# Both feed-forwards of an audio tower written out over all groups, and the fp4 weight work spread over groups 1 to 7

## The reference, cut to what matters

```python
# third stage, L0_ffn (w1q, w3q, w2q: weights rounded to -s, 0, s); x is a layer-normed row block
h1 = jnp.einsum('bsd,hd->bsh', x, w1q)          # 512 -> 1365
h3 = jnp.einsum('bsd,hd->bsh', x, w3q)
g = jax.nn.silu(h1) * h3
return jnp.einsum('bsh,dh->bsd', g, w2q)        # 1365 -> 512

# fifth stage, L1_ffn: I = 1408
nib = w[:, :, None] >> shifts & jnp.uint32(15)  # 8 fp4 codes in each int32
vals = _FP4_LUT[nib.astype(jnp.int32)]          # 0 .5 1 1.5 2 3 4 6 and their negatives
w_gu, w_down = vals * s_full                    # one scale per 128 inputs
gate_up = jnp.einsum('bsh,oh->bso', x, w_gu)
h = jax.nn.silu(gate) * up
y = jnp.einsum('bsi,hi->bsh', h, w_down)
return y / jnp.sqrt(jnp.mean(y * y, axis=-1, keepdims=True) + EPS)

h = h + _L0_ffn_ref(_layernorm(h, axis=-1), ...)
h = h + _L1_attn_ref(_layernorm(h, axis=-1), ...)
h = h + _L1_ffn_ref(_layernorm(h, axis=-1), ...)
```

## Time and profile before

| What | Value |
|---|---|
| Median of three runs | 2518.8 us (2515.69 to 2519.2) |
| The profiled execution | 2522.83 us, span 2521.0 us |
| TensorE matmuls busy | 2265.6 us, 90% of the span |
| VectorE busy | 1672.8 us, 66% |
| ScalarE busy | 1491.4 us, 59% |
| GpSimd busy | 994.3 us, 39% |
| Mean granted TensorE clock | 0.960 |

### The profile page before, as it was taken

How to read it: one execution, slowest core, us unless ns; L and a number is a source line. 1 busy time by engine, 2 the same in 40 slices (tenths; PEclk the granted TensorE clock), 3 DMA queues, 4 the chain that set the end, 5 groups by cost and what they waited for, 6 DMA issues and landing times. The chain is left out here.

```text
span 2521.0 us, 43883 instructions
## 1 busy us (share of the span) xinstructions
PE 2265.6 (90%) x13188; PEld 1136.4 (45%) x13188; DVE 1672.8 (66%) x2917; ACT 1491.4 (59%) x2374; POOL 994.3 (39%) x1002
## 2 busy tenths in 40 slices
PE   7999999987999992699999995999986999999997
PEld 2333333334666661344444442666652344444443
DVE  6666666655787875674444763666647888788873
ACT  4566666665777775573222653766745666666663
POOL 2222222246777770240000541444434545455552
PEclk9999999998999996899999997999998999999999
DMA  5555445424222210221121223222211111111101
GB/s 147 141 132 126 131 130 134 129 75 180 64 74 62 75 47 18 65 81 62 53 68 55 87 69 100 83 76 76 86 51 39 34 47 38 39 50 42 43 26 50
DMA packets 144174, 194.53 MB, mean 77 GB/s; under 512 B 32549, under 2 KB 76165, under 8 KB 144058
## 3 DMA queue, kind: packets, MB, share of 16 engines
q1 hardware_dynamic: 117754, 160.10, 20.9%
q10 hardware_dynamic: 26304, 33.04, 4.8%
HBM read 125.17 MB, written 42.21 MB: 66 GB/s over the span
## 5 line engine op out<-in xcount | busy, mean ns | idle before, releaser
L337 DVE TENSOR_REDUCE tm_negmax<-tm_s 128x1 f32<-128x512 f32 x512 | 323.3, 678 | 169.7 <-PE tm_s L380 169.4
L299 ACT ACTIVATE tm_prob<-tm_s 128x1024 f32<-128x1024 f32 x256 | 257.4, 1023 | 137.3 <-PE tm_s L400 132.8
L2217 PE MATMUL f_part<-f_xhi,gu 128*128 128x512 f16 x704 | 271.4, 385 | 14.2 <-ACT f_firstg L2038 3.9
L2217 PE MATMUL f_part<-f_xlo,gu 128*128 128x512 f16 x704 | 270.2, 384 | 0.0
L417 PE MATMUL tm_o<-tm_prob,tm_vt 128*64 128x512 f32 x1024 | 257.4, 623 | 0.0
L2239 PE MATMUL f_pz<-dn,f_ghi 128*128 128x512 f16 x704 | 217.8, 385 | 27.0 <-ACT f_zc L2070 27.0
L2007 POOL TENSOR_TENSOR f_firstg<-f_firstg,f_secondg 128x512 f32<-128x512 f32 x88 | 148.6, 1688 | 198.2 <-DVE f_secondg L2113 198.2
L380 PE MATMUL tm_s<-tm_qk 96*128 96x512 f16 x512 | 199.7, 392 | 14.5 <-DMA tm_qk<-tm_xs 14.0
L260 POOL TENSOR_TENSOR tm_hn<-tm_nd,tm_rows 128x1024 f32<-128x1024 f32 x32 | 75.2, 2350 | 313.6 <-DMA tm_rows<-rden 313.6
L400 PE MATMUL tm_s<-tm_qk 98*128 98x512 f16 x512 | 194.9, 384 | 4.3 <-DMA tm_qk<-tm_mrow 4.3
L962 PE MATMUL a_bankB<-a_wo,a_yThi 128*128 128x512 f16 x512 | 156.2, 387 | 4.4 <-DVE a_yTlo L885 4.3
(11 more groups left out here) (190 smaller groups left out, 5728.4 us busy)
## 6 DMA issues: line engine op xcount, KB each, us to landing
tm_qk<-tm_xs SPq DMA_DIRECT2D x384, 64.0 KB, 2.1
tm_xqk<-in_qk ACTq DMA_DIRECT2D x32, 512.0 KB, 4.6
a_hin<-h SPq DMA_DIRECT2D x64, 256.0 KB, 2.6
a_hres<-h SPq DMA_DIRECT2D x64, 256.0 KB, 3.1
h<-a_hout SPq DMA_DIRECT2D x64, 256.0 KB, 2.5
f_hin<-h SPq DMA_DIRECT2D x64, 256.0 KB, 2.7
f_hres<-h SPq DMA_DIRECT2D x64, 256.0 KB, 2.7
tm_vt<-in_vt ACTq DMA_DIRECT2D x32, 256.0 KB, 2.9
```

The lines of the kernel that those rows point to most:

```text
L299: nc.scalar.activation(prob[b][:, 2 * h:2 * h + 2, :], s2[:, i % 2, :, :], ACT.Exp, scale=SCALE).then_inc(exp_done, 1)
L337: nc.vector.tensor_reduce(negmax[u][:, m:m + 1], s1[:, p % BANKS, :], AX.X, ALU.max, negate=True).then_inc(s1_read, 1)
L2217: last = nc.tensor.matmul(part[q % BANKS][:, :], (gate, up)[which][:, j, m * P:(m + 1) * P], xparts[x][u][:, j, :], start=x == 0, stop=x == 1)
```

## The change

Three things change.

1. FROM and TO are both set to the number of groups in both feed-forwards, and `loop_pairs` leaves the loop out where it is empty. All steps become straight code, with constants in their waits.
2. `slot` no longer asks which groups stand outside the loop. Group 0 gets no fp4 work. In groups 1 to 7 every second block begins a chunk: the even m in the groups 1, 3, 5 and 7, the odd m in the groups 2, 4 and 6.
3. Nothing else: the number of chunks, their operations, all buffers and the order within a block stay as they are.

```diff
@@ loop_pairs
     for n in range(first, loop_from):
         step(n // 2, n % 2)
-    with eng.Fori(loop_from // 2, loop_to // 2) as k:
-        step(k, 0)
-        step(k, 1)
+    if loop_from < loop_to:
+        with eng.Fori(loop_from // 2, loop_to // 2) as k:
+            step(k, 0)
+            step(k, 1)
@@ feed_forward, slot
-        full = [g for g in range(GROUPS) if not FROM <= g < TO]
-        if beside is None or not isinstance(n, int) or n not in full:
+        if beside is None or not 1 <= n < GROUPS:
             return None
-        at = full.index(n) * MT + m
-        return None if at % 7 == 6 else at - at // 7
+        at = (n - 1) * MT + m
+        return None if at % 2 else at // 2
@@ feed_forward
-        FIRST, FROM, TO, LAST = -1, 2, (GROUPS - 1) // 2 * 2, GROUPS + 1
+        FIRST, FROM, TO, LAST = -1, GROUPS, GROUPS, GROUPS + 1
@@ feed_forward_fp4
-        FIRST, FROM, TO, LAST = -1, 2, (GROUPS - 1) // 2 * 2, GROUPS + 2
+        FIRST, FROM, TO, LAST = -1, GROUPS, GROUPS, GROUPS + 2
```

## The result

The changed kernel takes 2493.15 us (median of four runs, 2491.76 to 2497.36), the kernel before 2519.0 (four runs, 2515.69 to 2522.49): a ratio of 0.9899, interval 0.9887 to 0.9912, or 25.9 us less. I read the profiled execution of the changed kernel, 2493.78 us with a span of 2491.8.

What follows compares the result with a forecast made beforehand. TensorE's products were taken to bound the loop's groups, the ScalarE and VectorE chain group 0. The terms -13.7 - 2.8 - 0.1 + 3.2 - 0.7 + 2.8 - 4.0 - 2.2 gave -17.5, from 2518.8 to 2501.3 us, range 2494 to 2511.

Steps and rivals of the forecast that it cites:

- Group 0: First feed-forward: without fp4 work group 0 runs at TensorE's pace, 41.3 us instead of 55.0, a gain of 13.7.
- The half clock behind its end: After group 0 of the first feed-forward: the f_xlo wait's backlog goes and the half clock with it, 2.8 us less.
- the end of group 1: First feed-forward, end of group 1: a small gain of 0.1 us in the sum.
- The group ends: First feed-forward: fp4 work at m = 9 delays f_xlo; groups 2 and 4 lose 1.6 us each, group 6 gains 0.7.
- the third blocks: First feed-forward: fp4 work at m = 10 makes the next group's third block wait; groups 3 and 5 add 2.8 us together.
- rival A: First feed-forward: group ends lose 2.5 us each, half followed by half clock, +11 us, so 2512; chance 0.15.
- The start of group 7: First feed-forward: the third block's wait of 2.5 us and 1.5 us of half clock behind it go, 4.0 less.
- The loops: Loop turns: nothing in the first feed-forward; the second loses its branch, 2.2 us less; 1.5 us of half clock left open.
- C: Both feed-forwards: straight code starves on instruction fetches, 12 stops of 2.1 us, so slower at 2526; chance 0.03.
- D: First feed-forward: group 0 stays bound by the chain, only 4 of 13.7 us return, half clock stays, 2514; chance 0.05.
- B: More half clock goes in the second feed-forward (4.5 us), new group ends lose nothing (6 us), 2491 to 2497; chance 0.14.

Runs made afterwards that it cites:

- experiment 1: The changed kernel with the second feed-forward back in its loop, so only the first is straight code with the new fp4 places: 2498.78 us, ratio 0.9922.
- experiment 3: The kernel before with the first feed-forward as straight code but fp4 work still in groups 0, 1, 6 and 7: 2516.14 us, ratio 0.9993.
- 9: The kernel before, unchanged, profiled once more: 2521.96 us.
- experiment 2: The kernel before with only the second feed-forward written out as straight code: 2512.28 us, ratio 0.9977.
- experiment 6: The changed kernel with fp4 chunks kept out of blocks m = 9 and m = 10 of each group: 2484.99 us, ratio 0.9864.
- 10: The changed kernel, unchanged, profiled once more: 2491.57 us.
- 11: The kernel before with only the second feed-forward written out, unchanged from its first run, profiled once more: 2514.09 us.
- experiment 7: The changed kernel with ScalarE's copy f_zc and its squares ahead of a step's last hidden_hi in the second feed-forward: 2476.17 us, ratio 0.9831.

## Why the prediction was wrong, and where it was right

**Group 0** (−13.7): right. It became 12.6 us shorter. TensorE's pace and full blocks are there; the missing 1.1 us are the half clock at its start, which held for 5.4 us of group 0 and not for 3. In the second profile it held for 2.7, and the group lasts 41.1. The half clock behind its end and the end of group 1 (−2.8 and −0.1) came: group 1 takes 58.74 us instead of 61.66 (60.67 in the second profile of before, where that stretch was half as long).

**The group ends** (+3.2 − 0.7) and **the third blocks** (+2.8): right in place and nearly in size. An f_xlo wait is 1.62 us by starts where 1.6 was said. The f_prod waits are 1.31 and 1.68 where 1.4 each was said, and the one kept for group 2 (0.8) is gone; that the narrow chunk's smaller delay fits is likely, but no run changed it alone. By group, against before: +0.7, 0.0, +3.0, 0.0 and +1.0 for groups 2 to 6.

The Trainium skill's rule on the shared SBUF interfaces ("GPSIMD Engine Reference", "Specifications") is borne out by f_glo again, at 0.69, 1.19 and 1.57 us. The code, sign and join steps at m = 9 took 0.68 to 0.69 with no GpSimd work beside them, so rival A's step that they stretch there did not occur. They can: a sign step of the changed kernel (1371.97 us) took 1.53 beside a GpSimd multiplication.

**The start of group 7** (−4.0): −4.5 in the first pair of profiles; −3.0 in the second, where before's half clock fell ahead of that wait and shortened it. Here the close agreement of the first pair is in part luck. The eight groups together, to the wait for the last f_glo, give −15.3 us in the first pair of profiles and −15.4 in the second: the sum's own number. In both pairs the stage gains another 1.3 or 1.4 us behind that, where a half-clock stretch of before is shorter or gone; this end was not in the sum.

**The loops** (−2.2): this is the step that failed. The branch was right: 4.57 us became 2.54. (The 2.54 are 0.15 more than the 2.39 that the prediction expected, and the whole groups are shorter all the same.) The sentence "These 1.5 us may return or not; I leave them in the range" failed. It counted the half clock behind one wait at zero, although by its own rows the half clock stood behind the long wait, which was to go, and not behind the one of 2.39, and the other stretches of the stage not at all, although they stand in before's trace. Between the first and the sixth of these waits, in the first pair of profiles:

| Term | Working | us |
|---|---|---|
| branch at the turn | 4.57 − 2.54 | −2.0 |
| half clock behind the waits at 2045, 2192, 2339 | 3 x 1.7 | −5.1 |
| groups of the loop a little longer (71.97 against 71.71) | about 3 x 0.26 | −0.8 |
| sum | | −7.9 |
| measured | (2382.68 − 2024.11) − (2410.95 − 2044.53) | −7.9 |

The other 1.6 us of the stage's 9.4 (9.44 − 7.85) lie ahead of the first and behind the sixth wait. In the second pair one stretch stays in this piece and the difference is 6.4. Over all profiles this piece lasts 366.1 us in the loop (366.42, 366.62, 364.76 and 366.61 in before, 1, 3 and 9) and 359.6 in straight code (358.57, 360.25, 358.56, 360.22 and 360.21 in after, 2, 6, 10 and 11): 6.5 less, of which about 2.1 are the branch and 0.8 the groups, so that some 3.6 are left for half clock. Between 3 and 5 us of half clock, not zero, belonged into the sum; with 0.8 for the groups and 5 for the half clock the sum would have been near −17.5 − 0.8 − 5 = −23. The stretch behind the turn goes with its long wait: it stands there in all four profiles of the loop and in none of the five of straight code. That the other stretches became fewer is what the profiles show; that the change did it is not shown, since experiment 3 has none of them in the loop.

**What the sum left out.** The medians split the miss of 8.4 us in two: experiment 1 gained 19.2 where its terms give 15.3, and experiment 2 gained 5.7 where the loops' term gives 2.2. The first excess is not in the eight groups, which came out at the sum's number; 1.3 or 1.4 us lie at the stage's end, and for the rest the profile shows an earlier start of group 0, a place that the sum put at nothing without a word.

**Rivals.** A is refuted by experiment 6: the new ends cost 8 us, as summed, and no half clock. C is refuted by experiment 3 and by the missing stops at new code (ScalarE's "issue" is gone, and VectorE's is a wait for GpSimd); the Trainium skill's rule on fetches ("Runtime: NRT & Kernel Launch", "Instruction fetch mechanics"), by which sequential code is fetched ahead, agrees: 2.08 us at the branch, none in its place. No run tells the fetch from the rest of what the branch costs. D is refuted by group 0's 42.4 us. B held for the half clock alone: 2493.15 lies in its span of 2491 to 2497, but its group ends that lose nothing were wrong, and the earlier start of group 0 took their place. That is luck.

**What stays open.** In both profiles the changed kernel reaches group 0 some 4 us earlier, in stages that the change does not touch. 1.4 us of it are there from the first product on, at 12.5 and 12.6 us, before at 14.0 and 13.9. That goes with the program: all seven profiles of kernels with both feed-forwards written out have it between 12.5 and 13.1 us, all six with a loop in one or both between 13.9 and 15.2. What makes the first transfers land sooner was not tried. The rest, 2 to 3 us, builds up over the first 700 us; it is not explained. Half clock ahead of group 0 fits the first pair (102.9 us of it before, 90.2 after) and not the second (97.0 and 99.7). Over all 13 profiles group 0 starts between 1017.8 and 1023.0 us in the nine whose first feed-forward is written out, and between 1024.4 and 1025.1 in the four where it is a loop; so this start, too, may go with the program. And why a 2.54 us wait is followed by half clock in one case and not in the next is not explained: waits of equal length did both, so that length alone does not decide, although the longest (4.6 to 4.8 us) always had it behind them and those of 0.47 us never.

## What to carry to other kernels

Before a change that shifts a repeated wait by a few tenths of a us, list every stretch at half clock in the stage, not only the one beside the edit, in more than one profile, since their number differs between executions. Put their price (here 1.7 us each) into the sum, as a range: the loop here had one to four, the straight code none or two. Deferrable work beside a stage goes where the matrix engine has cover (a projection) and is kept out of the blocks whose last result opens the next group: experiment 6 gains 8 us by choice of places alone. And when a wait repeats at every group start, look at what stands ahead of the releasing instruction on its own engine: moving one copy and its square ahead of one cast was worth 17 us, two thirds of the whole change.

## What the runs showed of the hardware that was not expected

- Waits of one length, 2.54 us, in the same code, were followed by 1.2 GHz in some cases and 2.4 GHz in others: behind none and one of six in two profiles of the changed kernel, behind three of six with five more products in each group, behind one with 16 more. Waits of 0.47 us (experiment 7) were followed by none, the four of 4.6 to 4.8 us at the loop's turn (before, experiments 1, 3 and 9) all by 1.2 GHz.
- An f_glo of 128 or 85 rows by 512 took 0.69 us alone, and 1.19 to 1.57 beside a GpSimd multiplication of 1.26 us: GpSimd's work cost VectorE up to 0.88 us, which was longer than the operation itself. The cost depends on when the two meet: the stretched operations all ended 0.54 or 0.55 us behind the end of the multiplication.
- A group of the second feed-forward took 71.71 us as straight code and 71.97 in the loop, where the counts of the waits come from registers. What of the loop makes the 0.26 us was not tried.
